# Layer 0 of a conditioned four-layer stack: only the visible keys are scored, kind by kind over four heads

## The reference, cut to what matters

```
def _sparse_mask(T):                       # BLOCK_SIZE = 128, WINDOW = GLOBAL_EVERY = 64
    idx = jnp.arange(T)
    blk = idx // BLOCK_SIZE
    future_block = blk[None, :] > blk[:, None]
    outside_window = jnp.abs(idx[None, :] - idx[:, None]) > WINDOW
    global_visible = jnp.broadcast_to((idx % GLOBAL_EVERY == 0)[None, :], (T, T))
    return outside_window & ~global_visible | future_block
...
c_kv = h @ Wkd.T
k = (c_kv @ Wku.T).reshape(B, T, N_KV_HEADS, HEAD_DIM).transpose(0, 2, 1, 3)
v = (c_kv @ Wvu.T).reshape(B, T, N_KV_HEADS, HEAD_DIM).transpose(0, 2, 1, 3)
...
scores = jnp.einsum('bhtd,bhsd->bhts', q, k_exp) / jnp.sqrt(jnp.asarray(HEAD_DIM, x.dtype))
scores = jnp.where(mask[None, None], jnp.asarray(-jnp.inf, x.dtype), scores)
attn = jax.nn.softmax(scores, axis=-1)
y = jnp.einsum('bhts,bhsd->bhtd', attn, v_exp)
out = y.transpose(0, 2, 1, 3).reshape(B, T, C) @ Wo.T
return x + out
```

## Time and profile before

| | us |
|---|---|
| median of 3 runs | 2461.66 |
| lowest, highest | 2458.26, 2464.49 |
| profiled execution, its own time | 2457.0 |
| its span | 2455.2 |
| PE busy | 2316.3 (94%) |
| DVE, ACT, POOL busy | 1214.6, 1071.1, 292.4 |
| first scores of layer 0 start at | 92.53 |

### The profile page before, as it was taken

How to read it: one execution, slowest core, us unless ns; L and a number is a source line. 1 busy time by engine, 2 the same in 40 slices (tenths; PEclk the granted TensorE clock), 3 DMA queues, 4 the chain that set the end, 5 groups by cost and what they waited for, 6 DMA issues and landing times.

```text
span 2455.2 us, 33197 instructions
## 1 busy us (share of the span) xinstructions
PE 2316.3 (94%) x13384; PEld 1516.3 (62%) x13384; DVE 1214.6 (49%) x2486; ACT 1071.1 (44%) x2417; POOL 292.4 (12%) x246
## 2 busy tenths in 40 slices
PE   6889999999999999999999989999998989999998
PEld 2444455455555587888877756565564568888633
DVE  2465565544546454443444265757477554544332
ACT  2465565544435331111113356657567652222373
POOL 3331121120211110200001010101010120000021
PEclk8899999999999999999999999999999999999999
DMA  9200000000001011210101212111110010000001
GB/s 297 93 17 17 1 17 27 10 1 9 9 1 44 9 56 39 91 65 26 35 7 60 80 50 70 35 53 44 55 41 13 26 32 35 18 18 1 0 18 52
DMA packets 54009, 96.48 MB, mean 39 GB/s; under 512 B 9456, under 2 KB 23040, under 8 KB 53856
## 3 DMA queue, kind: packets, MB, share of 16 engines
q1 hardware_dynamic: 52880, 91.85, 11.4%
q0 software_dynamic: 976, 2.51, 0.3%
HBM read 77.83 MB, written 10.49 MB: 36 GB/s over the span
## 4 chain that ended last, share of the span: by engine, by line
PE 84%; DVE 7%; ACT 6%; POOL 1%; issue 1%; DMA 0%; SPq 0%; DVEq 0%; POOLq 0%; ACTq 0%
PE banks L1080 35%; PE banks L403 21%; PE banks L693 8%; PE banks L685 6%; PE banks L709 5%; DVE sb_Pr L765 2%; ACT sb_Pr L795 2%; PE banks L265 1%; PE banks L719 1%; PE banks L441 1%; PE banks L591 1%; DVE sb_hN L364 1%; ACT sb_PT L800 1%; PE banks L509 1%; PE banks L599 1%; ACT sb_t L303 1%
## 5 line engine op out<-in xcount | busy, mean ns | idle before, releaser
L1080 PE MATMUL banks<-sb_HH,sb_Ws 128*128 128x512 f32 x1536 | 490.2, 393 | 12.8 <-DVE sb_HL L970 7.3
L693 PEld LDWEIGHTS banks<-sb_ident,sb_Pr 128*128 128x128 f32 x2176 | 240.6, 142 | 204.5 <-issue 73.9
L693 PE MATMUL banks<-sb_ident,sb_Pr 128*128 128x128 f32 x2176 | 315.0, 282 | 36.1 <-DVE sb_PT L772 11.3
L1080 PEld LDWEIGHTS banks<-sb_HH,sb_Ws 128*128 128x128 f32 x1536 | 289.8, 189 | 77.3 <-issue 17.2
L795 ACT ACTIVATE sb_Pr<-sb_Pr,sb_nmax 128x512 f32<-128x512 f32 (+3 forms) x512 | 321.7, 635 | 22.1 <-DVE sb_nmax L765 22.1
L1080 PE MATMUL banks<-sb_hidH,sb_Ws 128*128 128x512 f32 x1024 | 331.2, 393 | 0.0
L765 DVE CUSTOM_DVE_ANT_0 sb_Pr<-banks,sb_bias 128x512 f32<-128x512 f32 (+3 forms) x512 | 273.5, 587 | 85.1 <-PE banks L685 81.0
L1080 PE MATMUL banks<-sb_HL,sb_Ws 128*128 128x512 f32 x768 | 300.1, 391 | 0.0
L800 ACT ACTIVATE sb_PT<-banks 128x512 f32<-128x512 f32 (+3 forms) x320 | 154.2, 528 | 317.5 <-PE banks L693 316.8
L772 DVE COPY sb_PT<-banks 128x512 f32<-128x512 f32 (+3 forms) x320 | 181.1, 603 | 175.4 <-PE banks L693 174.8
L1080 PEld LDWEIGHTS banks<-sb_hidH,sb_Ws 128*128 128x128 f32 x1024 | 192.3, 188 | 45.1 <-issue 3.8
(11 more groups left out here) (140 smaller groups left out, 2839.1 us busy)
## 6 DMA issues: line engine op xcount, KB each, us to landing
sb_ring<-split_units SPq DMA_DIRECT2D x48, 512.0 KB, 3.3
sb_staged<-in_L_cond_Wfc SPq DMA_DIRECT2D x16, 512.0 KB, 4.3
sb_wada<-in_L_cond_Wada SPq DMA_DIRECT2D x6, 1024.0 KB, 5.8
split_units<-sb_unitpair SPq DMA_DIRECT2D x12, 512.0 KB, 3.4
sb_x<-in_x SPq DMA_DIRECT2D x4, 1024.0 KB, 9.9
sb_staged<-in_L_cond_Wg SPq DMA_DIRECT2D x8, 512.0 KB, 3.6
sb_staged<-in_L_cond_Wu SPq DMA_DIRECT2D x8, 512.0 KB, 4.7
sb_staged<-in_L_cond_Wd SPq DMA_DIRECT2D x8, 512.0 KB, 4.3
```

The lines of the kernel that those rows point to most:

```text
L693: mm = e.transpose(bank[:, j * P:(j + 1) * P], k.Pr[:, n % 6, j * P:(j + 1) * P], k.ident[:])
L1080: mm = e.matmul(bank, lhsT, rhs, start=i == 0, stop=i == len(mats) - 1)
```

## The change

`NearHeads` takes the place of `Heads` in layer 0. It scores three kinds of keys per unit: `scores` (own tile, 128 columns), `before` (the 64 positions before it) and `far` (every 64th key up to there: 1, 3 or 5). The last two exist for i > 0, and lie side by side in the unit's bank: width 128 for i = 0, else 193, 195, 197. All four heads of a quad do one kind, then all the next. The mask becomes `mask0`, 200 columns per tile in the same order of keys; `exp` and `max` keep their form at the smaller width. A unit has one turn of 128 columns and, for i > 0, one of 65, 67 or 69, copied together to `PT`. `values` uses `V01` for the own tile and `VN` for the rest. `VN` (per batch 69 rows x 3 tiles x 128) holds the values of those other keys in their order: an eighth group of `proj0` computes it from the latent in six products and a DVE copy. What waited for group 6 or 5 as the latent's last reader now waits for group 7, and the first values too. The DMA of the mask brings 0.4 MB, not 1 MB. The other layers run the code they had.

```
+    def score_ops(s, b, quad):
+        kinds = ("scores", "before", "far") if s.units[quad[0]][2] else ("scores",)
+        return [(s, b, "pe", kind, u) for kind in kinds for u in quad]
...
+    def width(s, u):
+        i = s.units[u][2]
+        return 3 * P // 2 + 2 * i - 1 if i else P
...
+            mm = e.matmul(bank[:, 0:P], q, kk[rows, i * P:(i + 1) * P], start=True, stop=True)
...
+            mm = e.matmul(bank[:, P:P + 64], s.q(b, c)[rows, i * P:(i + 1) * P], kk[rows, i * P - 64:i * P],
+                          start=True, stop=True)
...
+            mm = e.matmul(bank[:, P + 64:s.width(u)], s.q(b, c)[rows, i * P:(i + 1) * P],
+                          kk[rows, 0:128 * i - 127:64], start=True, stop=True)
...
+            mm = e.transpose(bank[:, 0:P], prob[:, 0:P], k.ident[:])
+            if s.units[u][2]:
+                mm = e.transpose(bank[0:s.width(u) - P, P:2 * P], prob[:, P:s.width(u)], k.ident[:])
...
+            for half in range(2):
+                i = 2 * ip + half
+                queries, others = slice(half * P, (half + 1) * P), 64 + 2 * i - 1
+                for hl in range(s.per):
+                    mm = e.matmul(bank[hl * s.dv:(hl + 1) * s.dv, i * P:(i + 1) * P], s.v(b, i, s.vhead(c, hl)),
+                                  s.PT[:, n % 2, hl, 0, queries], start=True, stop=i == 0)
+                for hl in range(s.per) if i else ():
+                    mm = e.matmul(bank[hl * s.dv:(hl + 1) * s.dv, i * P:(i + 1) * P],
+                                  s.near(b, i, s.vhead(c, hl))[0:others, :], s.PT[0:others, n % 2, hl, 1, queries],
+                                  start=False, stop=True)
...
-        for h, b, u in units(t + 1):
-            seq.append((h, b, "pe", "scores", u))
+        for h, b, u in units(t + 1)[0:1]:
+            seq.extend(h.score_ops(b, range(u, u + 4)))
...
-                         lambda b: [("proj0", b - 1, "mm", 6)] if b else [],
+                         lambda b: [("proj0", b - 1, "mm", 7)] if b else [],
...
+            for i in range(1, TT):
+                o, ready = slice((i - 1) * P, i * P), [("proj0", b, "put", 0)]
+                mats.append(((slice(0, 64), o), latent[:, i * P - 64:i * P], wvu, True, True, ready))
+                mats.append(((slice(64, 63 + 2 * i), o), latent[:, 0:128 * i - 127:64], wvu, True, True, ready))
...
+            Group(near_values, "dve", lambda e, b, bank: e.tensor_copy(
+                VN[0:69, b % 2, :, :], bank[0:69, 0:3 * P].rearrange("p (i m) -> p i m", i=3)), free=v_free("heads0"))])
...
-                    e.dma_start(k.bias[:], a["mask0"].rearrange("(i p) t -> p i t", p=P)).then_inc(l_bias[0], 16)
+                    e.dma_start(mask0[:], a["mask0"].rearrange("(i p) t -> p i t", p=P)).then_inc(l_bias[0], 16)
```

More of the change, by code:

```diff
@@ L402, in pe @@
                     e.wait_ge(*due)
-            mm = e.matmul(bank[:, columns], lhsT, rhs, start=start, stop=stop)
+            out = bank[:, columns] if isinstance(columns, slice) else bank[columns]
+            mm = e.matmul(out, lhsT, rhs, start=start, stop=stop)
         mm.then_inc(k.done["pe"], 1)
@@ L664, in width, with scored @@
         return P * s.tiles_of(s.units[u][2])
+    def score_ops(s, b, quad):
+        return [(s, b, "pe", "scores", u) for u in quad]
+    def scored(s, u):
+        return "scores"
     def column(s, c, i, hl):
@@ L756, in dve @@
         if kind == "max":
-            for due in after(s.name, b, "scores", u):
+            for due in after(s.name, b, s.scored(u), u):
                 e.wait_ge(*due)
@@ L820, in seated @@
             if isinstance(stage, Heads):
+                if kind in ("before", "far"):
+                    continue
                 if kind == "scores":
@@ L1352, in conditioned_stack @@
         LAST = 4 * NCH - 1
-        scores_end = lambda name, b: [(name, b, "scores", last_unit[name])]
+        scores_end = lambda name, b: [(name, b, "far" if name == "heads0" else "scores", last_unit[name])]
         values_end = lambda name, b: [(name, b, "values", 7)]
```

85 lines of the change are left out of this document (73 added, 12 removed).

## The result

| | before | after |
|---|---|---|
| median, us (4 runs each) | 2461.99 | 2437.82 |
| lowest, highest | 2458.26, 2464.49 | 2433.65, 2442.23 |
| ratio | | 0.9903, 95% interval 0.9879 to 0.9928 |
| profiled execution, its own time | 2457.0 | 2433.65 |
| first scores of layer 0 at | 92.53 | 94.65 |

The account below looks back on a forecast made before the run. The prediction took PE to bound the kernel: -35 us in layer 0's heads, +5.7 for the added group, +3.6 at the start, +1 for side work, about -25 us in total; forecast 2435 us, range 2420 to 2450.

Follow-up runs that it names:

- experiment 1: The kernel after the change, with each head scoring all its kinds of keys before the next head does: 2480.85 us, ratio to before 1.0072.

## What to carry to other kernels

Where three engines hand a unit on in turn, cutting the work of the busiest alone buys in part a wait; ask of each saved instruction whether the step that it waits for next gets shorter too, and price the relief of the others as a term of its own. Neighbouring small products should be written so that heads on different strips alternate, one kind at a time, and a column more in one product is cheaper than a product more (by the rows, 64 columns cost 0.10 us when they lengthen the product of 128 and 0.22 as a product of their own, four heads together). An added group belongs where the engine waits for a transfer anyway.

## What the runs showed of the hardware

- Four heads' fp32 products on four strips of 32 rows run side by side only if they stand next to each other: a quad's twelve products (24 records) take 0.77 us kind by kind, 1.75 us head by head.
- A second product of 1 to 5 columns on each strip costs 0.11 us for the four (0.65 against an estimated 0.54 for 192 columns in one kind, between the 0.44 and 0.65 us of 128 and 256), a third kind 0.12.
- In a stage that keeps PE 92% busy the granted clock falls beside waits of PE of 2.0 to 2.6 us, at four such waits in one execution and at two of the same four in another, 1.7 us short of full clock each time. Not every fall has such a wait: three in experiment 1 have none of 1 us.
- In the lead the place where the clock goes up moves the first score by 5.5 us from execution to execution, and the time short of full clock in the rest of the program moves its length by 13 us (1984 to 1997). Span times mean granted clock takes most of this out: 25 executions of one kernel between 2452 and 2468 us agree to a standard error of 0.4 us.
